# Cutting the carry in the decay tiles on ScalarE instead of in the step sizes on GpSimd, in a two-direction selective scan

## The reference

```python
xn = layernorm(x)
# selective scan, once forward and once over the reversed tokens with weights of its own
dbc = xn @ x_proj_w.T                        # 32 values for delta, 16 for B, 16 for C
delta = softplus(dbc[..., :32] @ dt_proj_w.T + dt_proj_b)
deltaA = exp(delta[..., None] * -exp(A_log)) # 16 states for each channel
BX = delta[..., None] * B[:, :, None, :] * xn[..., None]
h[t] = deltaA[t] * h[t - 1] + BX[t]          # the scan, by an associative scan
y = sum_over_states(h * C) + D * xn
s = y_forward + y_backward
# an expert of 8 is chosen by a router from tokens' last row; row b uses expert sel[b]
out = (gelu(xn @ W1[sel] + b1[sel]) @ W2[sel] + b2[sel]) @ Wo + bo
x = x + s * silu(xn + 0.3 * out)
```

## Time and profile before

| | |
|---|---|
| time, median of 3 runs | 3178.7 us (3178.13 to 3183.46) |
| the profiled execution | 3178.13 us, span 3176.3 us |
| mean granted TensorE clock | 0.931 of full speed |
| DVE busy | 3068.3 us, 97% (of it 1024 scans of 2.28 us) |
| POOL busy | 3011.4 us, 95% (of it 608 bx of 2.38 us and 448 hc of 2.37 us) |
| ACT busy | 2900.1 us, 91% |
| PE busy | 2521.8 us, 79% |
| POOL's cut (L451) | 64 memsets, 6.8 us in all, 0.106 us each |
| DMA | 394 MB, mean 124 GB/s |

### The profile page before, as it was taken

The page is one execution under the profiler, slowest core; times in us unless marked ns, Lnnn a source line. Parts: engine busy times, 40 slices in busy tenths (PEclk is TensorE's granted clock), DMA queues, the critical chain, the costliest instruction groups (busy, mean ns, idle before and its releaser), DMA issues. The chain is left out here.

```text
span 3176.3 us, 48665 instructions
## 1 busy us (share of the span) xinstructions
PE 2521.8 (79%) x15766; PEld 2006.4 (63%) x15766; DVE 3068.3 (97%) x2027; ACT 2900.1 (91%) x5114; POOL 3011.4 (95%) x1486
## 2 busy tenths in 40 slices
PE   7778878888778888788887788887788777887886
PEld 5566656666666666566666566665666665666665
DVE  3899999999999999999999999999999999999999
ACT  4999999999999999999999999999999999999995
POOL 2899999999999999999999999999999999999997
PEclk9999999999999999999999999999999999999998
DMA  5443344444344433344433444433444333444331
GB/s 164 145 132 113 117 124 127 141 124 124 102 128 137 136 122 121 111 128 135 135 113 115 123 129 139 125 122 103 129 137 135 117 123 113 128 135 135 105 120 54
DMA packets 273362, 394.14 MB, mean 124 GB/s; under 512 B 45003, under 2 KB 119508, under 8 KB 273108
## 3 DMA queue, kind: packets, MB, share of 16 engines
q1 hardware_dynamic: 273108, 391.03, 40.4%
HBM read 348.98 MB, written 25.18 MB: 118 GB/s over the span
## 5 line engine op out<-in xcount | busy, mean ns | idle before, releaser
L480 POOL TENSOR_TENSOR bx<-dx,b_sb 128x1024 f32<-128x1024 f32 x608 | 1437.6, 2384 | 21.0 <-DVE hs L861 20.8
L861 DVE TENSOR_TENSOR_SCAN hs<-decay,bx 128x1024 f32<-128x1024 f32 x608 | 1384.7, 2282 | 15.1 <-issue 8.0
L1093 PE MATMUL y<-ident,hc 128*128 128x128 f32 x8192 | 1107.8, 285 | 36.7 <-DVE hc L840 36.7
L1093 PEld LDWEIGHTS y<-ident,hc 128*128 128x128 f32 x8192 | 989.9, 147 | 142.3 <-DVE hc L840 95.2
L468 POOL TENSOR_TENSOR hc<-hs,c_sb 128x1024 f32<-128x1024 f32 x448 | 1057.2, 2371 | 18.1 <-DVE hs L861 17.4
L861 DVE TENSOR_TENSOR_SCAN hs<-decay_sb,decay 128x1024 f32<-128x1024 f32 x416 | 937.4, 2273 | 15.5 <-issue 12.6
L736 ACT ACTIVATE decay<-delta,rate 128x512 f32<-128x512 f32 x1216 | 790.0, 687 | 99.7 <-DVE hs L861 99.0
L594 ACT ACTIVATE dxb<-dxT,btok 128x256 f32<-128x256 f32 x1664 | 710.1, 504 | 0.0
L840 DVE TENSOR_TENSOR hc<-hs,c 128x1024 f32<-128x1024 f32 x576 | 690.6, 1199 | 1.5 <-PE c L1076 0.7
L1068 PE MATMUL decay<-ident,dxb 128*128 128x128 f32 x3328 | 457.3, 282 | 243.7 <-DVE hs L861 231.7
L1068 PEld LDWEIGHTS decay<-ident,dxb 128*128 128x128 f32 x3328 | 379.7, 144 | 375.5 <-issue 302.3
(11 more groups left out here) (125 smaller groups left out, 2045.9 us busy)
## 6 DMA issues: line engine op xcount, KB each, us to landing
b_sb<-b_scratch SPq DMA_DIRECT2D x608, 256.0 KB, 3.3
c_sb<-b_scratch SPq DMA_DIRECT2D x448, 256.0 KB, 3.6
xin<-in_L_attn_x_dram SPq DMA_DIRECT2D x32, 512.0 KB, 6.4
w_sb<-in_L_ffn_W_dram SPq DMA_DIRECT2D x32, 512.0 KB, 3.4
w2o_sb<-w2o_scratch SPq DMA_DIRECT2D x32, 512.0 KB
xres<-in_L_attn_x_dram SPq DMA_DIRECT2D x32, 512.0 KB, 5.3
out_dram<-og SPq DMA_DIRECT2D x32, 512.0 KB, 4.4
dbc<-high SPq DMA_DIRECT2D x64, 128.0 KB, 2.3
```

The costliest lines, as they stand in the source:

```text
L480: nc.gpsimd.tensor_tensor(bx[:, i % RING, :, :], dx[:, g, :, :], b_sb[:, i % BRING, :].unsqueeze(1).broadcast_to([P, DT, T]), ALU.mult).th ...
L861: V.tensor_tensor_scan(hs[:, s % HSLOTS, :, :].rearrange("p k t -> p (k t)")[:, u], factor.rearrange("p k t -> p (k t)")[:, u], data.rearr ...
L1093: ins = M(yps[:, c, k * P:(k + 1) * P], hc[:, s % RING, k, c * P:(c + 1) * P], ident[:, :], start=False, stop=(s == ADDED[-1]), is_transpo ...
```

## The change

The cut moves from delta to the decay tiles. An Identity on ACT with scale 0 writes a column of zeros into a decay tile (cut_of), and the two exps leave that column out, so that a slot keeps its zero column from one use to the next. The column is written anew only where the slot is new to the group (a turned step's first use of each of the three SBUF slots in a group: steps 5, 6, 8, 22, 24, 26) or has been overwritten by other data since (EDGED, for the two PSUM tiles: steps 0, 1, 7, 10, 16, 17). That makes 12 cuts a row. The scan of such a step waits for one more semaphore. The memsets on POOL, their wait and the lower bound of the rates go; make_decay waits for s_delta.

Four pieces of the order change too: POOL's residual stands at step 3 instead of 4; the decay of step 30 is no longer made ahead at step 26, but at 28; and on ACT the copy of the second turned half of dx (step 31) stands before the decay of the next row's step 1 instead of after it. The copy at step 30 stays where it was.

```diff
@@ -39,12 +39,12 @@
     B_TURN, B_COPY = 11, 13
     EXPAND, ABS = (14, 15, 24, 25), (16, 17, 26, 27)
     EXP, LN, SQUARE, RATIO = (18, 27), (19, 28), (20, 29), (21, 30)
-    LOG1P, STEPSIZE, DX, CUT = (25, 36), (27, 39), (28, 43), (29, 44)
+    LOG1P, STEPSIZE, DX = (25, 36), (27, 39), (28, 43)
     DX_TURN, DX_COPY = (28, 29, 44, 45), (30, 31, 46, 47)
     FFN_IN, HIDDEN, GELU = (16, 16, 18, 18, 20, 20, 22, 22), (18, 20, 22, 24), 31
     FFN_OUT, GATE = (31, 31, 32, 32, 34, 34, 35, 35), (35, 38)
     FFN_OUT_FIRST, GATE_FIRST = (33, 33, 34, 34, 36, 36, 37, 37), (36, 38)
-    Y_OUT, Y_RESIDUAL = 1, 4
+    Y_OUT, Y_RESIDUAL = 1, 3
     SKIP = {0: ((0, 0), (2, 0)), 1: ((0, 1), (1, 0), (1, 1), (2, 1)), 4: ((3, 0), (3, 1))}
 
     TURNED, SCALED_AT, TURN_LEAD = (5, 6, 8, 9, 11, 13, 14, 15, 22, 24, 26, 28, 30), (1, 2, 3, 4, 5, 7, 9, 10, 17, 19, 21, 23, 25), 3
@@ -54,9 +54,10 @@
     NT, NBX, ND, NPC = len(TURNED), len(POOL_B), len(ON_DVE), len(POOL_C)
     ADDED = [s for i in range(STEPS + ADD_LAG) for s in ((i - ADD_LAG,) if i - ADD_LAG in POOL_C else ()) + ((i,) if i in ON_DVE else ())]
     FIRST_TURNED = [next(i for i, s in enumerate(TURNED) if s >= g * N) for g in range(2)]
-    NO_CARRY, LEAST_RATE = 1e20, 1e-16
-
-    AHEAD, AHEAD_NEXT = {14: 22, 15: 24, 16: 26, 23: 28, 26: 30}, {}
+    EDGED_SB = [s for s in TURNED if TURNED.index(s) - FIRST_TURNED[s // N] < TSLOTS]
+    EDGED = [s for s in POOL_B if s % N < DSLOTS or s - DSLOTS in TURNED]
+
+    AHEAD = {14: 22, 15: 24, 16: 26, 23: 28}
     EPS = 1e-5
 
 
@@ -203,7 +204,8 @@
         s_proj, s_bstored = sem("projected_copied"), sem("b_stored")
         s_bsb, s_bx = [sem(f"b_loaded{i}") for i in range(BRING)], sem("bx_done")
         s_decay, s_scan, s_cps, s_hc, s_red = (sem(n) for n in ("decay_done", "scan_done", "c_psum", "hc_done", "sum_states_done"))
-        s_cut, s_diag, s_decay_sb = sem("delta_cut"), sem("skip_diagonal"), sem("decay_turned_done")
+        s_edge, s_diag = sem("segment_edges"), sem("skip_diagonal")
+        s_edge_sb, s_decay_sb = sem("segment_edges_turned"), sem("decay_turned_done")
         s_csb, s_hcp = [sem(f"c_loaded{i}") for i in range(CRING)], sem("hc_pool_done")
         s_bturn, s_btok = sem("b_turned"), sem("b_tokens_copied")
         s_dxturn, s_dxT = sem("dx_turned"), sem("dx_tokens_copied")
@@ -444,12 +446,6 @@
                 wait(pool, s_dxturn, (row - 1) * 2 * DT + g * DT + DT)
                 nc.gpsimd.tensor_tensor(dx[:, g, :, :], delta[:, g * (1 + par), :, :], xnT[:, par, :, :], ALU.mult).then_inc(s_dx, 1)
 
-            def cut(row, par, g):
-
-                pool.wait_ge(s_dx, row * 2 + g + 1)
-                later, edge = (1, 0) if g == 0 else (0, T - 1)
-                nc.gpsimd.memset(delta[:, g * (1 + par), later, edge:edge + 1], NO_CARRY).then_inc(s_cut, 1)
-
             def log1p(row, g):
                 pool.wait_ge(s_ratio, row * 2 + g + 1)
                 nc.gpsimd.tensor_tensor(lg[:, :, :], lg[:, :, :], ex[:, g, :, :], ALU.mult).then_inc(s_log1p, 1)
@@ -508,14 +504,11 @@
                     step_size(row, par, STEPSIZE.index(s))
                 if s in DX:
                     step_x(row, par, DX.index(s))
-                if s in CUT:
-                    cut(row, par, CUT.index(s))
 
             shift_of(0)
             log1p(0, 0)
             step_size(0, 0, 0)
             step_x(0, 0, 0)
-            cut(0, 0, 0)
 
             def body(row, par, last):
                 for s in range(STEPS):
@@ -733,21 +726,33 @@
             copy_dxT(0, 1)
             def decay_of(row, par, s, to, k):
                 g, n = s // N, s % N
-                return A(to[:, k, :], delta[:, g * (1 + par), k, :], ACT.Exp, scale=rate[:, g, k, n:n + 1])
+                later = 1 - g
+                cols = slice(0, T) if k != later else slice(1, T) if g == 0 else slice(0, T - 1)
+                return A(to[:, k, cols], delta[:, g * (1 + par), k, cols], ACT.Exp, scale=rate[:, g, k, n:n + 1])
+
+            def cut_of(s, to):
+                later, edge = (1, 0) if s < N else (0, T - 1)
+                return A(to[:, later, edge:edge + 1], eps[:, :], ACT.Identity, scale=0.0)
 
             def make_decay(row, par, s):
 
-                act.wait_ge(s_cut, row * 2 + s // N + 1)
+                act.wait_ge(s_delta, row * 2 + s // N + 1)
                 if s in TURNED:
                     i = row * NT + TURNED.index(s)
                     used = i - TSLOTS
                     wait(act, s_scan, used // NT * STEPS + TURNED[used % NT] + 1)
+                    to = decay_sb[:, i % TSLOTS, :, :]
+                    if s in EDGED_SB:
+                        cut_of(s, to).then_inc(s_edge_sb, 1)
                     for k in range(DT):
-                        decay_of(row, par, s, decay_sb[:, i % TSLOTS, :, :], k).then_inc(s_decay_sb, 1)
+                        decay_of(row, par, s, to, k).then_inc(s_decay_sb, 1)
                 else:
                     wait(act, s_scan, row * STEPS + s - DSLOTS + 1)
+                    to = dps[s % DSLOTS]
+                    if s in EDGED:
+                        cut_of(s, to).then_inc(s_edge, 1)
                     for k in range(DT):
-                        decay_of(row, par, s, dps[s % DSLOTS], k).then_inc(s_decay, 1)
+                        decay_of(row, par, s, to, k).then_inc(s_decay, 1)
 
             act.wait_ge(s_rate, 1)
             act.wait_ge(s_w2oc, 2 * NE - 2)
@@ -763,17 +768,15 @@
                 for s in range(STEPS):
                     if s in AHEAD:
                         make_decay(row, par, AHEAD[s])
-                    if s in AHEAD_NEXT and not last:
-                        make_decay(row + 1, 1 - par, AHEAD_NEXT[s])
                     drain(row, par, s + STEPS)
-                    if not last and s not in DX_COPY[:DT]:
+                    if not last and s != DX_COPY[0]:
                         drain(row + 1, 1 - par, s)
                     if s + DSLOTS < STEPS:
-                        if s + DSLOTS not in AHEAD.values() and (row == 0 or s + DSLOTS not in AHEAD_NEXT.values()):
+                        if s + DSLOTS not in AHEAD.values():
                             make_decay(row, par, s + DSLOTS)
                     elif not last:
                         make_decay(row + 1, 1 - par, s + DSLOTS - STEPS)
-                    if not last and s in DX_COPY[:DT]:
+                    if not last and s == DX_COPY[0]:
                         drain(row + 1, 1 - par, s)
                     if s in SCALED_AT:
                         scale_dx(row, par, SCALED_AT.index(s))
@@ -846,11 +849,15 @@
                 if s in TURNED:
                     i = row * NT + TURNED.index(s)
                     dve.wait_ge(s_bxT, i + 1)
+                    if s in EDGED_SB:
+                        dve.wait_ge(s_edge_sb, row * len(EDGED_SB) + EDGED_SB.index(s) + 1)
                     dve.wait_ge(s_decay_sb, DT * i + DT)
                     data, factor = dps[s % DSLOTS][:, :, :], decay_sb[:, i % TSLOTS, :, :]
                 else:
                     i = row * NBX + on_bx(s)
                     dve.wait_ge(s_bx, i + 1)
+                    if s in EDGED:
+                        dve.wait_ge(s_edge, row * len(EDGED) + EDGED.index(s) + 1)
                     dve.wait_ge(s_decay, DT * i + DT)
                     data, factor = bx[:, i % RING, :, :], dps[s % DSLOTS][:, :, :]
                 used = s - HSLOTS
@@ -897,7 +904,7 @@
             low_part(0)
             dve.wait_ge(s_aexp, 1)
             V.tensor_scalar(rate[:, :, :, :].rearrange("p a k n -> p (a k n)"), rate[:, :, :, :].rearrange("p a k n -> p (a k n)"),
-                            -1.0, -LEAST_RATE, ALU.mult, ALU.min).then_inc(s_rate, 1)
+                            -1.0, None, ALU.mult).then_inc(s_rate, 1)
             V.tensor_tensor(dsum[:, :], dskip[:, 0, :], dskip[:, 1, :], ALU.add).then_inc(s_dsum, 1)
             dve.wait_ge(s_dsum, 1)
             for k in range(DT):
```

## The result

The changed kernel takes 3227.93 us (median of 4 runs, 3227.16 to 3228.38), the kernel before, in the same comparison, 3181.08 (3178.13 to 3184.03). The ratio is 1.0145, with a 95% interval of 1.0131 to 1.0158: slower by 46.9 us, where 3225 and 46.8 more were forecast.

The account below looks back on a forecast made before the run. DVE's queue was taken to set the end, with ACT setting scan 13; 0.95 + 0.66 - 0.10 = 1.51 us a row, x 31 = 46.8, on the profiled 3178.13 gave 3225 us, own range 3215 to 3238.

Parts of the forecast that it names:

- Who sets the row: ACT sets the moment of scan 13, DVE the rest; POOL follows with one real rest a row, 1.77 us.
- Second copy ahead of decay 1: On ACT at the row's turn: the copy now waits for PE's second turn, mean 0.95 us a row later.
- Six cuts: On ACT between PE's second turn and decay 13: six cuts at 0.11 us each, 0.66 a row.
- 0.10 taken up at decay 12: On ACT: decay 12 sometimes waits for scan 10, which takes up about 0.1 us of the shift.
- Where the stall shows: On DVE: about 0.95 us more ahead of scan 2, the rest of the shift ahead of scan 13.
- Residual at 3: On POOL: a 3.1 us wait, free while ACT's shift covers it, otherwise 0.75 us a row.
- 0.08 of handshake in the slack of hc 27: Ahead of scan 31: 0.54 us of slack after POOL's hc 27, of which 0.08 was taken as handshake.
- One more wait: On 12 of DVE's scans: the added semaphore wait was taken to cost 0.
- The upper bound of 1.0: On DVE: the most the added waits could cost, 0.08 us of lost overlap x 12 = 1.0 a row.
- Decay 30: On ACT, made at step 28: rests of 0.93 and 0.82 take the 1.24 us moved; no cost or gain.
- The sum of 1.51 a row: Delay of decay 13 and scan 13: 0.95 + 0.66 - 0.10 = 1.51 us, over 31 row changes 46.8.

Follow-up runs that it names:

- e12: Kernel before with ACT's second ratio at step 29 instead of 30 and the scaled dx of step 15 at step 11 instead of 10: 3153.84 us, -18.6.
- e4: Kernel before with only the second dx copy moved ahead of decay 1: 3211.00 us, 38.2 over before.
- e2: Changed kernel with POOL's residual back at step 4: 3227.84 us, 55.0 over before.
- e5: Kernel before with only POOL's residual at step 3: 3207.25 us, 32.8 over before.
- e1: Changed kernel with the second dx copy back behind decay 1: 3216.56 us, 43.7 over before.
- e6: Kernel before with twelve DVE scans each waiting once more, for a semaphore long reached: 3182.49 us, 8.0 over before.
- e8: Changed kernel with cuts and decays counted on one semaphore, so no scan has the added wait: 3226.69 us, 52.2 over before.
- e10: Kernel before with only the decay of step 30 made at step 28 instead of 26: 3164.64 us, -7.8 against before.
- e7: Changed kernel with another one-column Identity into a spare tile ahead of each cut: 3259.47 us, 87.0 over before.

## Why the prediction was right, and where it was not

- **Who sets the row.** Right: ACT's chain from PE's second turn to scan 13. e12 shows it from the other side, by taking work out of it.
- **Second copy ahead of decay 1: 0.95.** e4 by itself 1.00 (its table load comes 1.16 later, with 0.2 of PE's turn in it). The copy's new rest was as laid out (0.93 in the mean), but both of PE's turns ended later, as its slow stretch lies over them in more rows: 0.22 more, which the sum did not have. The table load behind decay 1 comes 1.26 later in the mean: 0.95, 0.22 and one cut of 0.09.
- **Six cuts: 0.66.** They measured 0.093 each to the next start, 0.56. The Trainium skill (Perfetto Trace Analysis, "Optimizing Scalar/DVE Operations") has about 93 ns for ScalarE on SBUF and says that the profiled latency is about twice that; the trace agrees, 0.093 and 0.189 (0.166 into PSUM). The page of the Trainium skill that the prediction cites (VectorE: DVE Perf Modes, "The TRN2 errata") has 224 cycles, 0.19, which is the duration here and not what the next instruction waits.
- **0.10 taken up at decay 12.** Together 0.95 + 0.22 + 0.56 = 1.73 against the 1.58 laid out at scan 13, so 0.15 was taken up on the way.
- **Where the stall shows.** The first half right (scan 2), the second wrong: scan 13 waits no longer than before. The rest of the shift came ahead of scan 1 (0.36), between scans 2 and 12 (0.30, most of it where DVE waits for PE ahead of the gate inputs), and at the low part ahead of scan 13 (0.17). The sum was right, as ACT still sets when scan 13 starts.
- **Residual at 3: nothing under cover, 0.75 without.** Right on both: e2 unchanged, e5 0.82 by its profile and 1.06 by time. The wait itself was 3.3 and not 3.1. The 0.08 of handshake in the slack of hc 27 stands in no row; in e1 a scan that POOL holds starts 0.03 behind a bx and 0.13 behind an hc.
- **One more wait: 0.** Wrong as a statement on DVE, 0.35 a row at scan 1 (e6, e8), right for the total, as ACT's chain covered it (e8: within 1.3 us of the changed kernel and of e2). The upper bound of 1.0 held.
- **Decay 30: nothing.** Wrong: e10 is 7.8 us faster. Decay 29 did come early enough to end a 0.09 wait. In the changed kernel scans 20 to 31 win back 0.15 a row, 0.10 of it at scan 29, which the sum did not have.
- The sum of 1.51 a row against 1.43 to 1.46: later turns, cheaper cuts and the gain from scan 20 on nearly cancel. That the total came out to 0.1 us is luck, and all the more so as the groups of the experiments put such a kernel 52 to 55 us over before. What held up is the chain, not the last digit.

## What to carry to other kernels

Lay two queues side by side at the place of an edit and find which of the other engine's instructions it now stands behind: moving a copy ahead of independent work cost 1.0 us a row or a little more, the 12 new instructions with their waits and the later decay 30 only 0.3 to 0.5. Two delays on different engines need not add: POOL waits for ACT once a row anyway, so ACT's delay gave POOL the time that its own wait took. Undoing the covered one alone shows nothing, so test the pair. On an engine that looks unbroken for 40 us, ask what could stand outside that stretch: two small moves gave 0.6%.

## What the runs showed of the hardware

One wait more on DVE, for a semaphore long reached, was hidden behind instructions of 0.7 to 2.3 us (e6, eleven scans a row), but cost 0.35 us behind four instructions that start 0.07 apart. A one-column Identity with a constant scale costs its queue 0.093 us, its pitch, and not its duration of 0.19. In the kernel before, the lower level of TensorE's clock came twice in each of 30 rows, once beginning 85 to 89 us behind scan 0, where PE was busy for 0.36 of the time, the least of the row. Where in the row such a stretch lay moved the end of PE's second turn by 1.4 us between rows of that one trace, and by 0.7 us in the mean between the changed kernel and e7.
